# A decoder layer on one core: the first norm by halves, its second half on ScalarE, and the rotary tables late

## The chip, the cores and the metric

The kernel runs on one core of one Trainium2 chip. The metric is the device time of one execution in microseconds (us); the time before is the median of three runs. Engines: PE is TensorE (its queue of weight loads is PEld), DVE is VectorE, ACT is ScalarE, POOL is GpSimd, SP is SyncE, whose queue issues the DMAs here.

## The reference

The input x has 8 sequences of 128 tokens with 256 features. The layer is, with residual sums between its parts:

```
h = layernorm(x)
attention with 16 heads of 128 and 64 memory slots per head:
  q, k = rope(h Wq^T), rope(h Wk^T);  v = h Wv^T;  g = h Wg^T
  s = clip(h Ws1^T Ws2^T + bs2);  es = exp(s);  enz = 1 / cumsum(es over tokens)
  A = tril(q k^T) / sqrt(128);  ok = enz * (A es);  qv = softmax(ok)
  o = tril((qv * enz) es^T) v;  rmsnorm(o) * silu(g), then Wo
cross attention, 32 heads of 8, with a rotary embedding by positions that are an input
feed-forward: 8 experts, the best 2 by a gate, and a shared one
```

Everything is computed in float32. A product with a weight is made of three fp32r products: each side is split into a rounded high part and a low part (high*high + high*low + low*high).

## The kernel before

The tokens stand as 8 sequences in two halves of 4. The program has three stages.

**Start-up.** SP issues twelve DMAs in order: the first half of x, the constants, the second half of x, the positions, `ws1`, `wqk[0]`, `ws2`, `wvg[0]` and others. DVE computes the statistics of both halves (`Norm.vector_stats`, L289), POOL takes variance to the power -1/2 (L313), and DVE normalises both halves (`vector_norm`, L304, 8 instructions of 128x256). PE transposes each half into two PSUM banks (L322, 8 transposes a half). ACT rounds each bank to `ht_hi` (`Norm.scalar`, L330, 4 instructions), and DVE subtracts to `ht_lo` (`vector_low`, L337, 4 instructions). While it waits, PE turns the identity over (`keep_clocked`, L526 to 529): 22 times, 6 times and 10 times. Then PE multiplies both halves by `Ws1` (the slot inputs, 6 matmuls of 512 columns a half), and DVE makes `us` out of each half: it adds the constants from PSUM into `u_full` (L723), rounds it (L725, a copy) and joins high and low part (L727). PE waits before ST and SN until all of `us` is there.

**The attention.** The 16 heads are 8 pairs. Pair i of the attention runs beside the projections of pair i+1. Projections ("fills") are QK n (queries or keys of one head and one half: 6 matmuls into one bank), VG n (values and gates of one sequence), ST, SN (slot scores) and CS (cumulative sums, with `Ln` and `Exp` on ACT). An attention group g has the steps A, E, T, W, O, OT, Y. Each engine walks through a list of steps written by hand. For the projections of pair 0 and the attention of pair 0 the lists are `H_PE`, `H_DVE`, `H_ACT` and `H_POOL` (L153 to 184); an entry (step, n, i) belongs to attention pair i, and i = -1 means the projections of pair 0. `every_turn` (L243) walks through the head list and then repeats `PE_ORDER`, `DVE_ORDER`, `ACT_ORDER`, `POOL_ORDER` in a loop for five further pairs. `head_plan` (L226) gives the first 14 fills one of 8 banks each, then two banks in turn. A fill waits until its bank's last content is drained: QK by three DVE instructions (L796 to 798), VG by two of ACT (L884, L887) and one of DVE (L803), ST and SN by one of DVE (L809), CS by ACT's `Ln` (`summed`). The loop's first QK waits for the first CS of the pair before.

Before the logarithm of CS 0, ACT loads the table set with `Ln` (L835), and after CS 1 it loads `exp_and_others` again (L917); `Tanh` and `Exp` are both in that set. L741 is DVE's part of A, L771 of OT, L673 and L680 are the matmuls of ST and SN.

**The rotary tables** of the cross attention, which comes after the eighth pair, are computed in the head: `RA` (DVE, 14 small instructions, L364 to 381), `RS` (ACT, one `Sin`, which needs a table set of its own, L385), `RT` (DVE, 4 small instructions, L391 and 392). RA is the first step of `H_DVE`, RS stands after VG 3 in `H_ACT`, RT after VG 4 in `H_DVE`.

**Cross attention and feed-forward** follow in an order written by hand; the change does not touch them.

Of the kernel before, what the change touches and what calls it, by code (L numbers as in the profile page):

```python
# [275 lines left out]
class Norm:  # L276


    def __init__(self, nc, ctx, banks, xs, hn, ht_hi, ht_lo, ident, name):
# [6 lines left out]
        self.half_set, self.rstd_done, self.hn_done = sem("half_set"), sem("rstd_done"), sem("hn_done")  # L286
        self.turned, self.hi_done, self.lo_done = sem("turned"), sem("hi_done"), sem("lo_done")

    def vector_stats(self, dve, x_in):  # L289
        for half in range(2):  # L290
            seqs = slice(4 * half, 4 * half + 4)
            dve.wait_ge(x_in[half], 16)
            for b in range(4 * half, 4 * half + 4):
                dve.bn_stats(out=self.stats[:, b, :], in_=self.xs[:, b, :]).then_inc(self.stats_done, 1)
            for b in range(4 * half, 4 * half + 4):
                dve.wait_ge(self.stats_done, b + 1)
                dve.bn_aggr(out=self.mv[:, b, :], in_=self.stats[:, b, :]).then_inc(self.mv_done, 1)
            dve.wait_ge(self.mv_done, 4 * half + 4)
            dve.tensor_scalar(self.var_eps[:, seqs, 0], self.mv[:, seqs, 1], EPS, None, ALU.add).then_inc(self.var_done, 1)
# [15 lines left out]
    def tensor(self, pe, normalised_here=True, before=lambda half: None):  # L315
        for half in range(2):
            before(half)
            if normalised_here:
                pe.wait_ge(self.hn_done, 4 * half + 4)
# [1528 lines left out]
```

## Time and profile before

| | us |
|---|---|
| median of 3 runs (604.08, 606.02, 606.09) | 606.02 |
| profiled execution, its own time | 605.02 |
| span in its profile | 603.2 |
| PE busy | 578.4 (96%) |
| DVE busy | 485.5 (80%) |
| ACT busy | 371.6 (62%) |
| POOL busy | 282.4 (47%) |

The span is the time from the first to the last instruction of that execution; 1.8 us lie around it. Busy time of an engine is the time in which an instruction of it runs; matmuls are pipelined, so a busy PE is not PE at its peak.

### The profile page before, as it was taken

The page shows a single profiled execution, that of the slowest core. Times are in us where ns is not written, and L with a number is a line of the kernel's source. Part 1 is how long each engine was busy: PE and PEld are TensorE (multiplying, and loading weights), DVE is VectorE, ACT ScalarE, POOL GpSimd, SP SyncE. Part 2 cuts the span into 40 slices and gives each one's busy share as a digit, 9 for nine tenths or more (in the row PEclk, how much of TensorE's full clock was granted, in tenths as well). Part 3 has the DMA queues.
Part 4 walks back from the last instruction along what each step waited for, and adds up shares of the span by engine and source line. Part 5 has one row for each costly group of instructions (what it writes and reads, how often), then busy time and mean ns, then how long its engine had stood idle before and what let it go on. Part 6 is the DMA issues. An engine that isn't in the chain of part 4 may idle for free. (4 is left out here: it accounts for less than half of the span.)

```text
span 603.2 us, 14152 instructions
## 1 busy us (share of the span) xinstructions
PE 578.4 (96%) x4426; PEld 487.8 (81%) x4426; DVE 485.5 (80%) x1150; ACT 371.6 (62%) x1168; POOL 282.4 (47%) x324
## 2 busy tenths in 40 slices
PE   6989999999999999999999999998799999999997
PEld 5868888888888888888888788886578878877786
DVE  6999978977977977986987888687597887886766
ACT  3438557657657566656655576776867567566453
POOL 3367754845754663664675566355771220220000
PEclk9999999999999999999999999999989999999999
DMA  8200201100100200200200000231000000000000
GB/s 274 74 0 11 80 1 35 54 2 25 62 0 0 87 0 0 87 0 0 87 0 0 18 3 1 89 120 76 2 3 11 4 10 12 3 10 13 3 9 18
DMA packets 10321, 19.35 MB, mean 32 GB/s; under 512 B 2336, under 2 KB 5920, under 8 KB 10144
## 3 DMA queue, kind: packets, MB, share of 16 engines
q1 hardware_dynamic: 10272, 18.74, 9.2%
q8 instruction: 26, 0.43, 0.3%
q14 instruction: 23, 0.19, 0.1%
HBM read 17.55 MB, written 1.05 MB: 31 GB/s over the span
## 5 line engine op out<-in xcount | busy, mean ns | idle before, releaser
L884 ACT ACTIVATE sa_v<-bank 128x256 f32<-128x256 f32 x64 | 24.5, 383 | 60.7 <-PE bank L268 60.7
L857 ACT ACTIVATE sa_ex<-sa_okb,sa_minus_top 128x64 f32<-128x64 f32 x128 | 43.0, 341 | 28.7 <-DVE sa_minus_top L750 26.7
L947 POOL TENSOR_TENSOR sa_qt<-sa_rope_cos,sa_rope_sin 128x512 f32<-128x512 f32 x32 | 41.1, 1286 | 39.0 <-DVE sa_rope_sin L798 38.1
L266 PE MATMUL bank<-ht_hi,sa_qk_hi 128*128 128x512 f32 x128 | 55.2, 431 | 1.4 <-DVE sa_gate L803 0.8
L947 POOL TENSOR_TENSOR sa_kt<-sa_rope_cos,sa_rope_sin 128x512 f32<-128x512 f32 x32 | 41.2, 1288 | 26.6 <-DVE sa_rope_sin L798 26.6
L266 PE MATMUL bank<-sa_vg_hi,ht_hi 128*128 128x512 f32 x128 | 53.0, 414 | 0.5 <-DVE sa_rope_sin L798 0.5
L268 PE MATMUL bank<-sa_vg_hi,ht_lo 128*128 128x512 f32 x128 | 50.5, 395 | 0.0
L267 PE MATMUL bank<-sa_vg_lo,ht_hi 128*128 128x512 f32 x128 | 50.5, 395 | 0.0
L268 PE MATMUL bank<-ht_hi,sa_qk_lo 128*128 128x512 f32 x128 | 50.5, 394 | 0.0
L796 DVE TENSOR_TENSOR sa_rope_cos<-bank,con 128x512 f32<-128x512 f32 x64 | 44.0, 687 | 7.8 <-PE bank L268 6.8
L267 PE MATMUL bank<-ht_lo,sa_qk_hi 128*128 128x512 f32 x128 | 50.2, 392 | 0.0
L1521 DVE TENSOR_REDUCE xf_neg_top<-bank 128x4 f32<-128x512 f32 x64 | 40.4, 683 | 9.4 <-PE bank L1399 9.4
L797 DVE TENSOR_TENSOR sa_rope_sin<-bank,con 64x512 f32<-64x512 f32 x64 | 44.4, 693 | 0.9
L798 DVE TENSOR_TENSOR sa_rope_sin<-bank,con 64x512 f32<-64x512 f32 x64 | 43.7, 684 | 0.8
L1722 POOL TENSOR_TENSOR xf_rot<-xf_by_cos,xf_by_sin 128x256 f32<-128x256 f32 x16 | 12.1, 759 | 61.2 <-DVE xf_by_sin L1514 61.2
L953 POOL TENSOR_TENSOR sa_qe<-sa_ex,sa_enz 128x256 f32<-128x256 f32 x32 | 23.5, 734 | 34.7 <-ACT sa_ex L857 34.7
L266 PE MATMUL bank<-sa_wo_hi,sa_ogt_hi 128*128 128x256 f32 x128 | 37.7, 295 | 0.7 <-issue 0.7
L1620 ACT ACTIVATE xf_wt<-bank 128x512 f32<-128x512 f32 x64 | 34.1, 603 | 6.5 <-PE bank L1411 6.5
L869 ACT ACTIVATE sa_junk<-bank 128x128 f32<-128x128 f32 x128 | 33.7, 283 | 6.6 <-PE bank L620 6.6
L764 DVE SCALAR_TENSOR_TENSOR sa_og<-bank,sa_rms,sa_gate 128x128 f32<-128x128 f32 x128 | 35.8, 343 | 1.6 <-POOL sa_rms L966 1.4
L803 DVE SCALAR_TENSOR_TENSOR sa_gate<-sa_th,bank 128x256 f32<-128x256 f32 x64 | 26.4, 417 | 12.5 <-ACT sa_th L887 5.9
L267 PE MATMUL bank<-sa_wo_lo,sa_ogt_hi 128*128 128x256 f32 x128 | 36.1, 282 | 0.0
(207 smaller groups left out, 1836.4 us busy)
## 6 DMA issues: line engine op xcount, KB each, us to landing
sa_qk_raw<-in_wqk SPq DMA_DIRECT2D x8, 512.0 KB, 3.8
sa_vg_raw<-in_wvg SPq DMA_DIRECT2D x8, 512.0 KB, 3.2
sa_wo_raw<-in_wo SPq DMA_DIRECT2D x8, 256.0 KB, 2.7
xf_w_raw<-in_w SPq DMA_DIRECT2D x2, 640.0 KB, 9.1
xf_w_raw<-in_w SPq DMA_DIRECT2D x1, 1152.0 KB, 7.4
xs<-in_x SPq DMA_DIRECT2D x2, 512.0 KB, 4.6
hn<-in_w SPq DMA_DIRECT2D x2, 512.0 KB, 4.8
out<-xs SPq DMA_DIRECT2D x8, 128.0 KB, 1.7
```

Source lines behind the costliest of these rows:

```text
L266: pe.matmul(out, w_hi, m_hi, start=first, stop=False)
L267: pe.matmul(out, w_hi, m_lo, start=False, stop=False)
L268: return pe.matmul(out, w_lo, m_hi, start=False, stop=last)
L764: ins = dve.scalar_tensor_tensor(out=og[:, s, u, :], in0=ps_o[s][:, u * DK:(u + 1) * DK], scalar=rms[:, s, u:u + 1], in1=gate[:, b, h * DK ...
L796: dve.tensor_tensor(rope_cos[:, s, :].rearrange("p (b t) -> p b t", b=4), psv, cos4, ALU.mult)
L797: dve.tensor_tensor(rs[0:64], psv[64:128], sin4[64:128], ALU.mult)
L798: dve.tensor_tensor(rs[64:128], psv[0:64], sin4[0:64], ALU.mult).then_inc(draining, 1)
L857: ins = act.activation(ex[:, s, u, :], okb[:, s, u, :], ACT.Exp, bias=minus_top[:, s, u:u + 1], accum_out=total[:, buffer_of(i, g, 4), u:u ...
L869: ins = act.activation(junk[:, u, :], ps_o[s][:, u * DK:(u + 1) * DK], ACT.Square, scale=(EPS * DK) ** -0.5, accum_out=ss[:, s, u:u + 1])
L947: pool.tensor_tensor(dst[:, h, c * HALF:(c + 1) * HALF], rope_cos[:, s, :], rope_sin[:, s, :], ALU.add).then_inc(roped, 1)
L1521: dve.tensor_reduce(neg_top[:, b % 2, n % 4, 4 * (n // 4):4 * (n // 4) + 4], bank(filled(step, n, b), 0, 512, 4), AX.X, ALU.max, negate=Tr ...
L1620: act.activation(wt[:, n, :, :], bank(filled(step, n, b), 0, 512, 4), ACT.Exp, scale=XDIM ** -0.5).then_inc(exp_done, 1)
```

## The change

The statistics are taken and normalised half by half, and the second half is normalised by ACT (`Identity` with scale rstd and bias -mean*rstd, the latter from one new DVE instruction). PE transposes the first half after 14 turns instead of 22, makes the first half's slot inputs, and only then transposes the second half; the second half's slot inputs come after QK 0 and QK 1. DVE's rounding copy of `us` goes to ACT. DVE takes QK 0 and QK 1 before VG 0 and VG 1. RA moves to after Y 0 of pair 0, RS to after VG 7 and before CS 0 of the projections of pair 1, RT to the end of DVE's head list. ACT loads its first table set before it waits for anything, and rounds `wvg[0]` before the second half's transposes instead of after `ws2`. ST and SN wait only for the two low parts of `us`.

```diff
-H_DVE = [("RA", 0, -1), ("VG", 0, -1), ("VG", 1, -1), ("QK", 0, -1), ("QK", 1, -1), ("VG", 2, -1), ("VG", 3, -1),
-    ("SN", 0, -1), ("SN", 1, -1), ("VG", 4, -1), ("RT", 0, -1), ("QK", 2, -1), ("QK", 3, -1), ("VG", 5, -1),
+H_DVE = [("QK", 0, -1), ("QK", 1, -1), ("VG", 0, -1), ("VG", 1, -1), ("VG", 2, -1), ("VG", 3, -1), ("SN", 0, -1),
+    ("SN", 1, -1), ("VG", 4, -1), ("QK", 2, -1), ("QK", 3, -1), ("VG", 5, -1), ("VG", 6, -1), ("QK", 4, -1),
...
+    ("VG", 2, 0), ("QK", 6, 0), ("W", 3, 0), ("O", 2, 0), ("VG", 3, 0), ("ST", 1, 0), ("Y", 0, 0), ("RA", 0, -1),
+    ("OT", 1, 0), ("VG", 4, 0), ("VG", 5, 0), ("OT", 2, 0), ("O", 3, 0), ("Y", 1, 0), ("QK", 7, 0), ("VG", 6, 0),
+    ("Y", 2, 0), ("OT", 3, 0), ("VG", 7, 0), ("Y", 3, 0), ("RT", 0, -1)]
-H_ACT = [("VG", 0, -1), ("VG", 1, -1), ("VG", 2, -1), ("VG", 3, -1), ("RS", 0, -1), ("W2P", 0, -1), ("VG", 4, -1),
+H_ACT = [("VG", 0, -1), ("VG", 1, -1), ("VG", 2, -1), ("VG", 3, -1), ("W2P", 0, -1), ("VG", 4, -1), ("W2P", 0, 0),
...
+    ("OT", 3, 0), ("VG", 7, 0), ("RS", 0, -1), ("CS", 0, 0), ("CS", 1, 0)]
...
+    def vector_shift(self, dve):
+        dve.wait_ge(self.rstd_done, 2)
+        dve.scalar_tensor_tensor(out=self.shift[:, :], in0=self.mv[:, 4:8, 0], scalar=-1.0, in1=self.rstd[:, 4:8, 0],
+                                 op0=ALU.mult, op1=ALU.mult).then_inc(self.shift_done, 1)
+    def scalar_norm(self, act):
+        act.wait_ge(self.shift_done, 1)
+        for b in range(4, 8):
+            act.activation(self.hn[:, b, :], self.xs[:, b, :], ACT.Identity, bias=self.shift[:, b - 4:b - 3],
+                           scale=self.rstd[:, b, 0:1]).then_inc(self.second_done, 1)
...
# tensor (PE)
-        norm.tensor(pe, before=lambda half: keep_clocked((22, 6)[half]))
-        keep_clocked(10)
-        pe.wait_ge(ws1_lo_done, 1)
-        for half in range(2):
+        keep_clocked(14)
+        norm.tensor(pe, 0)
+        keep_clocked(18)
+        pe.wait_ge(ws1_lo_done, 1)
+        slot_inputs(0)
+        norm.tensor(pe, 1)
+        keep_clocked(2)
...
         def head_waits(step, n, i):
+            if (step, n, i) == ("VG", 0, -1):
+                slot_inputs(1)
...
# vector (DVE)
-        norm.vector_stats(dve, x_in)
+        norm.vector_stats(dve, x_in, 0)
         norm.vector_norm(dve, 0)
-        norm.vector_norm(dve, 1)
+        norm.vector_stats(dve, x_in, 1)
         dve.wait_ge(ws1_hi_done, 1)
         dve.tensor_tensor(ws1_lo[:, :, :], ws1_raw[:, :, :], ws1_hi[:, :, :].bitcast(F32), ALU.subtract).then_inc(ws1_lo_done, 1)
+        norm.vector_shift(dve)
         norm.vector_low(dve)
...
+        def slot_low(half):
+            dve.wait_ge(us_hi_done, half + 1)
...
+        slot_sums(0)
+        def slot_inputs_too(step, n, i):
+            if (step, n, i) == ("QK", 1, -1):
+                slot_low(0)
+                slot_sums(1)
+            elif (step, n, i) == ("VG", 0, -1):
+                slot_low(1)
...
# scalar (ACT)
+        act.preload_act_table_set("exp_and_others")
         act.wait_ge(con_in, 16)
+        act.activation(tri_r[:, :], tri, ACT.Copy).then_inc(tri_done, 1)
         act.wait_ge(ws1_in, 16)
-        act.activation(tri_r[:, :], tri, ACT.Copy).then_inc(tri_done, 1)
         act.activation(ws1_hi[:, :, :], ws1_raw[:, :, :], ACT.Copy).then_inc(ws1_hi_done, 1)
+        norm.scalar(act, (0, 1))
         act.wait_ge(qk_in, 16)
         act.activation(qk_hi[:, :, :], qk_raw[:, :, :], ACT.Copy).then_inc(qk_hi_done, 1)
-        norm.scalar(act)
+        norm.scalar_norm(act)
+        act.wait_ge(vg_in, 16)
+        act.activation(vg_hi[:, :, :], vg_raw[:, :, :], ACT.Copy).then_inc(vg_hi_done, 1)
+        norm.scalar(act, (2, 3))
         act.wait_ge(ws2_in, 16)
         act.activation(ws2[:, :, :], ws2_raw[:, :, :], ACT.Copy).then_inc(ws2_hi_done, 1)
-        act.wait_ge(vg_in, 16)
-        act.activation(vg_hi[:, :, :], vg_raw[:, :, :], ACT.Copy).then_inc(vg_hi_done, 1)
+        for half in range(2):
+            cols = slice(half * HALF, (half + 1) * HALF)
+            act.wait_ge(u_full_done, half + 1)
+            act.activation(us[:, cols], u_full[:, cols], ACT.Copy).then_inc(us_hi_done, 1)
```

## Rows read from the trace of the kernel before

**Rows 1.** Stretches: length, busy us of PE, PEld, DVE, ACT, POOL, granted clock, DMA.

```profile
30.00:50.00 20.00, 18.28 (x95) 14.44 (x95) 19.49 (x37) 9.54 (x25) 13.48 (x11) 1.00 0.00 0
100.00:340.00 240.00, 237.76 (x1540) 204.18 (x1539) 198.92 (x401) 146.75 (x513) 139.94 (x151) 1.00 0.08 28
430.00:445.00 15.00, 12.52 (x118) 9.16 (x117) 9.51 (x31) 11.34 (x29) 7.94 (x10) 0.77 0.02 5
```

**Rows 2.** Timeline, PE, start-up: start, us, instruction, count.

```profile
5.67 4.96 PE L529 MATMUL bank<-con 128*128 128x128 f32 x22 [5.67 <-DMA con<-in_constants]
...
12.53 1.04 PE L322 MATMUL bank<-con,hn 128*128 128x128 f32 x8
...
14.42 0.48 PE L266 MATMUL bank<-ht_hi,sa_ws_hi 128*128 128x512 f32 x1
...
17.26 0.39 PE L266 MATMUL bank<-ht_hi,sa_qk_hi 128*128 128x512 f32 x1
```

**Rows 3.** Timeline, DVE, POOL and ACT, start-up.

```profile
6.28 1.02 POOL L313 TENSOR_TENSOR norm_rstd<-norm_var_eps,norm_minus_half 128x4 f32<-128x4 f32 x1 [4.96 <-DVE norm_var_eps L299]
...
7.61 1.40 DVE L294 BATCH_NORM_STATS2 norm_stats<-xs 128x6 f32<-128x256 f32 x4 [1.49 <-DMA xs<-in_x]
...
9.41 2.83 DVE L304 TENSOR_SCALAR hn<-xs,norm_mv,norm_rstd 128x256 f32<-128x256 f32 x8
9.58 1.25 POOL L313 TENSOR_TENSOR norm_rstd<-norm_var_eps,norm_minus_half 128x4 f32<-128x4 f32 x1 [2.28 <-DVE norm_var_eps L299]
...
9.84 0.40 ACT L820 ACTIVATE sa_ws_hi<-sa_ws_raw 128x256 fp32r<-128x256 f32 x1
...
12.49 2.60 DVE L337 TENSOR_TENSOR ht_lo<-bank,ht_hi 128x512 fp32r<-128x512 f32 x4
```

**Rows 4.** Timeline, DVE, the rounding copies of the slot inputs.

```profile
17.29 1.86 DVE L725 CAST sa_us<-sa_gate 128x512 fp32r<-128x512 f32 x1
...
20.63 0.43 DVE L725 CAST sa_us<-sa_gate 128x512 fp32r<-128x512 f32 x1
```

**Rows 5.** Timeline, PE and DVE, from 21.7 to 31.4 us.

```profile
21.77 0.67 DVE L364 TENSOR_TENSOR rotary_angle<-rotary_pos,con 128x4 f32<-128x4 f32 x8
...
23.77 0.75 DVE L803 SCALAR_TENSOR_TENSOR sa_gate<-sa_th,bank 128x256 f32<-128x256 f32 x2
...
28.40 1.07 PE L680 MATMUL bank<-sa_ws_pair,sa_us 128*128 128x128 f32 x8
...
29.35 1.28 DVE L809 TENSOR_SCALAR sa_sn<-bank 128x512 f32<-128x512 f32 x2
...
30.88 0.18 DVE L391 COPY rotary_cos<-rotary_trig 128x32 f32<-128x32 f32 x1
...
31.34 0.69 DVE L796 TENSOR_TENSOR sa_rope_cos<-bank,con 128x512 f32<-128x512 f32 x1
```

**Rows 6.** Timeline, DVE and PE, around Y 0 and OT 2 of pair 0.

```profile
79.33 0.68 DVE L771 TENSOR_TENSOR sa_ogt_lo<-bank,sa_ogt_hi 128x512 fp32r<-128x512 f32 x1
81.51 0.42 DVE L803 SCALAR_TENSOR_TENSOR sa_gate<-sa_th,bank 128x256 f32<-128x256 f32 x1 [1.50 <-PE bank L268]
...
81.80 0.60 PE L632 MATMUL bank<-con,sa_og 128*128 128x128 f32 x4
```

**Rows 7.** Timeline, ACT, the table loads and what runs on them.

```profile
26.49 1.28 ACT L385 ACT_TABLE_LOAD   x1
27.78 0.26 ACT L385 ACTIVATE rotary_trig<-rotary_angle 128x64 f32<-128x64 f32 x1
...
90.61 1.28 ACT L835 ACT_TABLE_LOAD   x1
91.90 0.60 ACT L909 ACTIVATE sa_log_cs<-bank 128x512 f32<-128x512 f32 x1
```

**Rows 8.** Timeline, PE, the loop's first QK, and a wait at 430 us.

```profile
92.90 0.48 PE L266 MATMUL bank<-ht_hi,sa_qk_hi 128*128 128x512 f32 x1
...
433.25 0.41 PE L1446 MATMUL bank<-con,hn 128*128 128x128 f32 x2 [2.41 <-DVE hn L1553]
```

More of the change, by code:

```diff
@@ L286, in __init__, with vector_stats @@
         self.half_set, self.rstd_done, self.hn_done = sem("half_set"), sem("rstd_done"), sem("hn_done")
+        self.shift, self.shift_done, self.second_done = sb("shift", [P, 4]), sem("shift_done"), sem("second_done")
         self.turned, self.hi_done, self.lo_done = sem("turned"), sem("hi_done"), sem("lo_done")
-    def vector_stats(self, dve, x_in):
-        for half in range(2):
[L291 to L299, printed above, removed]
+    def vector_stats(self, dve, x_in, half):
+        seqs = slice(4 * half, 4 * half + 4)
+        dve.wait_ge(x_in[half], 16)
+        for b in range(4 * half, 4 * half + 4):
+            dve.bn_stats(out=self.stats[:, b, :], in_=self.xs[:, b, :]).then_inc(self.stats_done, 1)
+        for b in range(4 * half, 4 * half + 4):
+            dve.wait_ge(self.stats_done, b + 1)
+            dve.bn_aggr(out=self.mv[:, b, :], in_=self.stats[:, b, :]).then_inc(self.mv_done, 1)
+        dve.wait_ge(self.mv_done, 4 * half + 4)
+        dve.tensor_scalar(self.var_eps[:, seqs, 0], self.mv[:, seqs, 1], EPS, None, ALU.add).then_inc(self.var_done, 1)
+    def vector_shift(self, dve):
[7 more added lines that the diff above has]
+                           scale=self.rstd[:, b, 0:1]).then_inc(self.second_done, 1)
     def vector_norm(self, dve, half):
@@ L313, in pool, with tensor, scalar @@
             pool.tensor_tensor(self.rstd[:, seqs, 0], self.var_eps[:, seqs, 0], self.minus_half[:, seqs], ALU.pow).then_inc(self.rstd_done, 1)
[L315 to L319, printed above, removed]
-            for kc in range(KC):
-                for b in range(4):
-                    mm = pe.transpose(self.banks[2 * half + kc][:, b * TOK:(b + 1) * TOK],
-                                      self.hn[:, 4 * half + b, kc * P:(kc + 1) * P], self.ident)
-                mm.then_inc(self.turned, 1)
-    def scalar(self, act):
-        for n in range(4):
+    def tensor(self, pe, half):
+        pe.wait_ge(self.second_done if half else self.hn_done, 4)
+        for kc in range(KC):
+            for b in range(4):
+                mm = pe.transpose(self.banks[2 * half + kc][:, b * TOK:(b + 1) * TOK],
+                                  self.hn[:, 4 * half + b, kc * P:(kc + 1) * P], self.ident)
+            mm.then_inc(self.turned, 1)
+    def scalar(self, act, steps):
+        for n in steps:
             half, kc = n // 2, n % 2
@@ L529, in keep_clocked, with slot_inputs @@
                 pe.transpose(banks[7][:, 0:TOK], ident, ident)
-        norm.tensor(pe, before=lambda half: keep_clocked((22, 6)[half]))
-        keep_clocked(10)
-        pe.wait_ge(ws1_lo_done, 1)
-        for half in range(2):
+        def slot_inputs(half):
             pe.wait_ge(norm.hi_done, 2 * half + 2)
@@ L718, in vector, with slot_sums @@
                                  in1=ws2_raw[:, :, :], op0=ALU.mult, op1=ALU.add).then_inc(ws2_done, 1)
-        for half in range(2):
+        def slot_sums(half):
             cols = slice(half * HALF, (half + 1) * HALF)
@@ L800, in run @@
                     dve.wait_ge(th_done, 8 * r + n + 1)
+                    if isinstance(r, int) and r == 0 and n == 0:
+                        dve.wait_ge(us_done, 2)
                     if attend:
@@ L809, in run @@
                     dve.tensor_scalar(dst[:, n, :], ps[:, :], -CLAMP, CLAMP, ALU.max, ALU.min).then_inc(draining, 1)
-        return every_turn(dve, H_DVE, run, banks, {"RA": lambda: rotary.vector_angles(dve), "RT": lambda: rotary.vector_tables(dve)})
+        return every_turn(dve, H_DVE, run, banks, {"RA": lambda: rotary.vector_angles(dve), "RT": lambda: rotary.vector_tables(dve)},
+                          before=slot_inputs_too)
     def scalar(act):
@@ L926, in gpsimd @@
         norm.pool(pool)
-        pool.wait_ge(norm.hn_done, SEQS)
+        pool.wait_ge(norm.hn_done, 4)
         pool.wait_ge(qk_hi_done, 1)
```

10 lines of the change are left out of this document (4 added, 6 removed), and 22 rows, old and new, of tables (H_ACT, H_DVE).

## The prediction

> **What bounds the kernel now.** I read the table of busy stretches first. From 100 to 340 us PE is busy 237.76 of 240 us [rows 1]: there the loop runs, nothing but PE's own work counts, and a delay of PE at its entrance stays to the end. From 30 to 50 us it is different: PE 18.28 of 20 us, DVE 19.49 [rows 1]. DVE sets the pace there and PE loses 1.72 us waiting for drained banks. So the change can win in two places: before 17.26 us, where PE has not yet begun its projections [rows 2], and in DVE's chain from SN 0 at 29.35 us on [rows 5], where what DVE has less to do moves everything behind it. It can lose wherever it puts work in front of something that PE is about to want. I then followed the timeline of each engine through the start, around 80 us and into the loop.
>
> **Part 1: PE's start.** DVE may normalise the first half as soon as POOL's power is done, 6.28 + 1.02 = 7.30 [rows 3]. One of the 8 instructions takes 2.83 / 8 = 0.35, four 1.42: done at 8.8 instead of 10.83. The 14 turns last 14 x 4.96 / 22 = 3.2 us from 5.67 [rows 2], to 8.8 also; so the first transposes start 2.0 us earlier, at 8.85 instead of 10.84. They run at the slow pace (8 x 0.22 = 1.8), to 10.6, and the 18 turns that follow fill PE to about 12.8. All this is ahead of what is needed, for the next step is held by something else: `vector_low` stands on DVE behind the new shift, the shift behind the second rstd. DVE's second statistics start at 8.8 instead of 7.61; from 7.61 to the variance at 9.50 it took 1.9 (POOL starts at 9.58), so POOL starts at 10.75 and needs 1.02 to 1.25 [rows 3]: 11.9. The shift is a 128x4 instruction that the trace does not have; at least 0.1 and at most the 0.35 of a normalising one, I take 0.2: 12.1. Two of the four low parts take 2 x 2.60 / 4 = 1.3 [rows 3]: 13.5. Then PE: slot inputs of one half, half of 17.26 - 14.42 = 2.84, so 1.42 to 1.47; second transposes 0.9 to 1.04 and two turns 0.2 [rows 2]. QK 0 starts at 13.5 + 1.45 + 0.95 + 0.2 = 16.1, between 15.9 and 16.4, against 17.26.
>
> But the second half's slot inputs have only moved behind QK 1, and they are 1.42 us. From QK 0 to SN 0 it was 28.40 - 17.26 = 11.14 [rows 2, 5]; now it is 12.56, and SN 0 starts at 28.65 instead of 28.40. PE has gained nothing by then: +0.25, between 0 and +0.6.
>
> ACT's new work hides. Four normalising activations of 128x256: nearest is 0.40 for a 128x256 copy [rows 3], so at most 1.6, more likely 1.2 with overlap and no less than half of that; 12.1 + 1.6 = 13.7, and PE wants them at 14.95. The cover is 1.2 us; behind the wait for the shift ACT has vg's rounding queued, which POOL's low part and VG 0 need, but VG 0 comes only at 16.1 + 2.8 + 1.4 = 20.3. ACT then still has the two banks and ws2 to round (an estimate from the 0.40 of 256 columns: under 1 us for 512, under 1.6 for 1024), which puts `slot_sums(0)` on DVE at about 19. The first table load is hidden before the constants arrive.
>
> **Part 2: DVE until SN 0.** What goes from DVE: four normalising instructions 1.42; the copies 1.86 + 0.43 = 2.29 [rows 4]; RA, 21.77 to 23.77 = 2.0; RT, 30.88 to 31.34 = 0.46 [rows 5]. That is 6.2 us. Laid out in the new order: sums of half 0 until 19.9, QK 0 (three of 0.69) 2.1 until 22.0, low part 0 and sums 1 until 23.4, QK 1 until 25.6, low part 1 26.2, VG 0 to 3 until 27.9 (each 0.33 by 0.75 for two, the later two waiting a little for ACT's `Tanh`). PE needs sums 1 for VG 3's bank at about 24.5, which leaves 1.1 us. In the kernel before DVE came to SN 0 at 29.35, just behind PE's SN 0 (half of it done at 28.40 + 0.6 = 29.0). Now DVE is there at 27.9 and waits for PE: 28.65 + 0.6 = 29.25. So of 6.2 us only what was behind 29.35 counts, RT's 0.46, and 0.1 by which SN is taken sooner, with 0.2 to either side for PE's start. QK 2 starts at 30.8 instead of 31.34 [rows 5] and the chain DVE to PE is 0.5 us earlier until PE takes over at about 46. Bounds: -0.2 and, if SN came as soon as DVE is free, -1.9. I take -0.5.
>
> **Part 3: RA at 79 us.** It stands in front of OT 1 (79.33) and takes 2.0. DVE was idle 1.50 us before the gate at 81.51 [rows 6], so most of it is hidden. OT 1 ends at 81.33 + 0.68 = 82.0 instead of 80.0; PE's OT 2 was at 81.80 [rows 6] and waits for it. +0.25; the gates and OT 2's own drain follow within that. At least 0 (if the POOL-free spot makes it shorter), at most +1.5 (if some of its copy-like instructions wait for POOL as the copy of 1.86 did against 0.43 [rows 4]).
>
> **Part 4: RS and RT at the loop's entrance.** Before, ACT loads Sin's table (1.28), runs Sin (0.26) and loads back (1.28) at 26.5, where ACT is not what is waited for. Now it stands between VG 7 and CS 0. One load is saved, since CS 0 loads its set anyway; the other is not: the load at 90.61 becomes Sin's, 1.28 and 0.26 later comes the one for `Ln` [rows 7]. The first logarithm ended at 91.90 + 0.60 = 92.50; now 94.06, 1.56 later. The loop's first QK on PE waits for exactly this (its bank) and started at 92.90 [rows 8], so 0.40 was to spare: PE stands 1.56 - 0.40 = 1.16. What follows it there (DVE's QK drain, A 1, E 0) moves with it, and the other late results of ACT (second logarithm, the pair's slot weights) are late by the same 1.56, so at most 0.4 more. Nothing gives it back, because the loop is PE's [rows 1]. Lower bound 0, if PE has other work to run ahead of the wait; the lists show none. RT hides behind this: DVE waits for Sin until about 92.2 with only the loop's A 0 queued behind it, and that needs PE's A 0, which ends just before 92.90. I take +1.15.
>
> The Trainium skill, "ScalarE: Activation LUTs", section "What ACT_TABLE_LOAD costs", says that a change of the table set costs 2.66 us, 1.28 for the load and about as much again for a drain. Here the load is 1.28 and the next activation starts 0.01 later (26.49, 1.28, 27.78) [rows 7]; by the page's figure the entrance would cost about 2.5 instead of 1.15 and the sum would be 1.4 higher. I go by the rows.
>
> **Sum.** -0.5 + 0.25 + 1.15 = +0.9. On the profiled execution, 605.02, it is 605.9; the median shown, 606.02, lies 1.0 above that execution and the lowest run 0.9 below it, so I predict between 605.9 and 606.9: 606.4.
>
> **Rivals.**
> (a) The likeliest, +0.9, with its own range from -0.5 to +2.2: 605 to 608. Chance 0.66.
> (b) DVE's relief carries through. The 6.2 us are really off an engine that was busy 19.49 of 20 us [rows 1], and if PE's QK 0 at 16.1 instead of 17.26 could be kept, PE's 1.72 us of waiting would go too. That gives up to -1.2 - 1.7 = -2.9, and with RT and a hidden Sin -3.4: 602.6. Against it: the 1.42 us of slot inputs only moved. Chance 0.05; half of it below 603.
> (c) The Sin is hidden at the loop's entrance or PE's wait is absorbed: -0.5 + 0.25 = -0.25, 605.3, decided by whether the first QK of the loop still starts 0.8 behind A 0. Chance 0.14.
> (d) Slower: PE's clock. The turns before 10.8 run at 4.96 / 22 = 0.23 each, the later transposes at 1.04 / 8 = 0.13 [rows 2], the two levels of 1.2 and 2.4 GHz. Later the granted clock falls for a while: mean 0.77 in 430 to 445 us, so 0.23 x 15 x 2 = 6.9 us at the lower level, after PE had stood 2.41 us [rows 1, 8]. In the new order PE waits once more in the start, some 0.7 us from 12.8 to 13.5. If that takes the clock away, or lets it rise later than now, everything up to SN 0 that falls in such a stretch runs at half pace: 3.4 us for 6.9. With +0.9 that is +4.3: 609.5 to 610.5. It decides from the point at which PE's wait comes near 2.4 us; I see 0.7 and no more than 1.3. The Trainium skill ("TensorE: Matmul & The Clock Gate", "What's actually happening") says the same in general, that the clock follows how busy the array has lately been; it gives no reason to expect a fall here. Chance 0.07.
> (e) RA meets POOL's work, and the late slot weights cost their 0.4: +0.9 + 1.3 + 0.4 = +2.6, 608.1. Chance 0.08.
> The stretches at the lower clock after 430 us may also fall otherwise once all is shifted by 1 us; that is the likely source of the 2 us between the three runs, and it goes into the range.
>
> **How the numbers follow.** 0.5% is 3.0 us, about what can be told from no change. Faster by more than that needs (b) whole: 0.04. Slower needs (d), or (e) with a bad run: 0.08. The rest, 0.88, is no change. The range that holds eight in ten is that of (a), (c) and (e) with 1 us of scatter between runs: 604.0 to 608.6.
>
> **What would show it.** PE's first transposes at 8.9, first slot-input matmul at 13.4 to 13.6, QK 0 at 16.1, SN 0 at 28.65; DVE idle about 1.3 us before SN 0 and QK 2 at 30.8; from there to 79 us each row 0.5 earlier. A wait of PE of about 0.2 before OT 2 of pair 0, and one of about 1.2 before the loop's first QK, released by ACT's logarithm, with an extra table load of 1.28 before it. The prediction is wrong if PE has no wait at the loop's entrance, if the low parts come well before 13.4, or if PE's clock falls before 30 us.

## The result and the profile after

The changed kernel took 606.26 us (median of 12 runs, 604.48 to 610.22) against 605.07 (602.63 to 606.09, 12 runs) for the kernel before: ratio 1.0037 with a 95% interval of 1.002 to 1.0054. Within 0.5% is what was predicted as "no change", and 606.26 lies 0.1 from the 606.4 of the forecast. The difference of the two medians is +1.2 us and the ratio says +2.2 (1.2 to 3.3 by its interval), where the sum said +0.9. That the time itself comes within 0.1 is partly luck: the forecast started from 605.5 (606.4 - 0.9) for the kernel before, which is 0.4 more than it now measures, and added 0.3 less than the medians show. The profiled execution took 606.32 us with a span of 604.5, against 605.02 and 603.2.

The stretches, as in [rows 1] (start and end; length; busy us and instructions of PE, PEld, DVE, ACT, POOL; granted clock; DMA share; GB/s):

```profile
30.00:50.00 20.00, 18.66 (x100) 14.89 (x98) 19.24 (x32) 9.82 (x24) 13.83 (x11) 1.00 0.00 1
100.00:340.00 240.00, 237.79 (x1543) 204.22 (x1542) 198.81 (x400) 147.63 (x520) 139.60 (x150) 1.00 0.08 28
422.00:430.00 8.00, 7.67 (x118) 5.89 (x116) 3.76 (x9) 5.45 (x13) 6.81 (x9) 0.57 0.00 0
430.00:445.00 15.00, 10.17 (x104) 7.23 (x103) 10.79 (x32) 12.75 (x33) 7.35 (x10) 1.00 0.01 3
```

In the loop nothing has changed (237.79 against 237.76 busy). From 30 to 50 us PE is busy 0.38 us more and DVE 0.25 less. The lower clock that the kernel before had from 430 to 445 us falls elsewhere in this execution: from 422 to 430 us the granted clock is 0.57, and from 430 to 445 it is 1.00, although PE stands there as long as it did before [rows 8], before this row of the timeline:

```profile
436.75 0.41 PE L1486 MATMUL bank<-con,hn 128*128 128x128 f32 x2 [2.40 <-DVE hn L1593]
```

The timeline of the changed kernel, rows of PE, DVE, ACT and POOL in the start, which answer to [rows 2, 3, 5] (start, us, engine, line, instruction, count, and in brackets the idle time before it and what ended it):

```profile
8.80 1.43 PE L332 MATMUL bank<-con,hn 128*128 128x128 f32 x8 [0.26 <-DVE hn L317]
...
11.78 0.16 DVE L304 SCALAR_TENSOR_TENSOR norm_shift<-norm_mv,norm_rstd 128x4 f32<-128x4 f32 x1 [0.91 <-POOL norm_rstd L326]
...
11.98 2.08 ACT L311 ACTIVATE hn<-xs,norm_shift,norm_rstd 128x256 f32<-128x256 f32 x4
12.01 2.37 POOL L969 TENSOR_TENSOR sa_qk_lo<-sa_qk_raw,sa_qk_hi 128x1024 fp32r<-128x1024 f32 x1 [0.27 <-ACT sa_qk_hi L857]
13.29 0.47 PE L266 MATMUL bank<-ht_hi,sa_ws_hi 128*128 128x512 f32 x1 [1.08 <-DVE ht_lo L347]
...
15.77 0.48 PE L266 MATMUL bank<-ht_hi,sa_qk_hi 128*128 128x512 f32 x1
...
25.02 1.85 POOL L987 TENSOR_TENSOR sa_kt<-sa_rope_cos,sa_rope_sin 128x512 f32<-128x512 f32 x1 [1.59 <-DVE sa_rope_sin L828]
...
28.37 0.89 PE L696 MATMUL bank<-sa_ws_pair,sa_us 128*128 128x128 f32 x7
28.96 1.29 DVE L841 TENSOR_SCALAR sa_sn<-bank 128x512 f32<-128x512 f32 x2 [1.19 <-PE bank L696]
...
30.50 0.68 DVE L826 TENSOR_TENSOR sa_rope_cos<-bank,con 128x512 f32<-128x512 f32 x1
```

QK 0 starts 1.49 us earlier than before, SN 0 only 0.03: the slot inputs of the second half stand between them. DVE is idle for 1.19 us before SN 0, so most of what was taken from it bought nothing. Its QK 2 is 0.84 earlier (31.34 before), but 5 us later its gate (L835, at 35.44) waits 0.28 for ACT's `Tanh`.

The same view later, PE, DVE, ACT and POOL, which answer to [rows 6 to 8]:

```profile
78.84 0.66 DVE L374 TENSOR_TENSOR rotary_angle<-rotary_pos,con 128x4 f32<-128x4 f32 x8
...
80.20 1.10 POOL L1006 TENSOR_TENSOR sa_rms<-sa_msq,sa_minus_half 128x4 f32<-128x4 f32 x1
80.21 0.23 DVE L385 SCALAR_TENSOR_TENSOR rotary_angle<-rotary_turns,rotary_angle 128x64 f32<-128x64 f32 x1
...
81.67 0.63 PE L648 MATMUL bank<-con,sa_og 128*128 128x128 f32 x4 [0.20 <-DVE sa_ogt_lo L801]
...
90.53 1.28 ACT L395 ACT_TABLE_LOAD   x1
91.82 0.26 ACT L395 ACTIVATE rotary_trig<-rotary_angle 128x64 f32<-128x64 f32 x1
92.09 1.28 ACT L875 ACT_TABLE_LOAD   x1
93.39 0.60 ACT L949 ACTIVATE sa_log_cs<-bank 128x512 f32<-128x512 f32 x1
...
94.12 0.50 PE L266 MATMUL bank<-ht_hi,sa_qk_hi 128*128 128x512 f32 x1 [1.06 <-ACT sa_log_cs L949]
```

PE's first QK of the loop starts at 94.12 instead of 92.90, behind two table loads in a row where there had been one.

To see where PE gains or loses, I set the start of each matmul against that of the same matmul of the kernel before (offset, in us; both profiled executions). For the changed kernel it is -0.09 at 30 us, -0.48 at 45, -0.10 at 83 (behind OT 2), +1.25 at 101 and +1.26 at 400. Behind 400 us the offset wanders by more than 2 us with the stretches at the lower clock, which fall differently in each execution; medians of 6 to 12 runs are therefore good to about 1 us, and the offset at 101 says more about the head.

### The profile page after: what moved, and what is told of

Its sections match the earlier page's. It is cut to its first block and busy times, and to the rows that moved or that the text cites. A ratio compares the mean times of both kernels' runs of the same rounds, so it can differ in the third digit from the quotient of the medians.

```text
span 604.5 us, 14143 instructions
## 1 busy us (share of the span) xinstructions
PE 577.0 (95%) x4422; PEld 485.8 (80%) x4422; DVE 481.7 (80%) x1145; ACT 373.2 (62%) x1173; POOL 282.4 (47%) x324
## 3 DMA queue, kind: packets, MB, share of 16 engines
HBM read 17.55 MB, written 1.05 MB: 31 GB/s over the span
## 5 line engine op out<-in xcount | busy, mean ns | idle before, releaser
L268 PE MATMUL bank<-sa_wo_hi,sa_ogt_lo 128*128 128x256 f32 x128 | 36.1, 282 | 0.0
```

The source lines that it names most:

```text
L268: return pe.matmul(out, w_lo, m_hi, start=False, stop=last)
```

## The experiments

All offsets in one place (PE against the kernel before, as above), with the times:

| kernel | at 30 | 45 | 83 | 101 | median us (range, runs) | ratio to before |
|---|---|---|---|---|---|---|
| changed, first | -0.09 | -0.48 | -0.10 | +1.25 | 606.26 (604.48 to 610.22, 12) | 1.0037 [1.002, 1.0054] |
| changed, again | +3.49 | +3.11 | +3.51 | +4.86 | 608.07 (604.13 to 612.9, 12) | 1.006 [1.003, 1.0089] |
| e1 rotary early | +6.97 | +7.75 | +7.73 | +7.73 | 612.15 (607.51 to 613.1, 6) | 1.0115 [1.0084, 1.0147] |
| e2 only rotary late | -0.30 | -0.69 | -0.26 | +1.05 | 605.75 (603.99 to 606.56, 12) | 1.0023 [1.0008, 1.0038] |
| e3 rotary hidden | +1.65 | +1.28 | +1.27 | +1.27 | 608.45 (607.32 to 610.0, 6) | 1.0078 [1.0055, 1.0101] |
| f1 POOL waits for shift | -0.01 | -0.40 | 0.00 | +1.33 | 606.67 (604.13 to 608.02, 12) | 1.0039 [1.0024, 1.0053] |
| f2 no sine table | +0.41 | +0.02 | +0.42 | +0.44 | 605.5 (602.99 to 606.61, 12) | 1.0011 [0.9996, 1.0026] |
| f3 best of changed | -0.05 | -0.44 | -0.46 | -0.46 | 604.57 (602.3 to 606.44, 12) | 0.9995 [0.9979, 1.0011] |
| f4 rotary covered, on before | -0.43 | -0.81 | -0.83 | -0.83 | 604.18 (602.52 to 605.3, 12) | 1.0003 [0.9989, 1.0016] |
| g1 low parts first | -0.34 | -0.70 | -0.70 | -0.68 | 605.07 (601.98 to 606.14, 12) | 1.0003 [0.9983, 1.0023] |
| h1 shift behind POOL | +2.48 | +2.11 | +2.10 | +2.10 | 604.52 (602.31 to 607.36, 12) | 1.0007 [0.999, 1.0025] |
| i1 rounding back on DVE | +2.08 | +1.69 | +2.07 | +3.41 | 608.29 (606.44 to 609.31, 6) | 1.0066 [1.0041, 1.0091] |
| j1 held but clocked | +3.20 | +2.80 | +3.23 | +4.56 | 608.97 (606.87 to 609.96, 10) | 1.0073 [1.0054, 1.0092] |

**The changed kernel again.**

> The changed kernel once more, as the measure for the others of this call. Theory (the time was lost at two places, in front of the loop and before OT 2, and only half a microsecond was won before): +1.3 us on the kernel before, rows from 100 us on later by 1.2 to 1.3; the first QK of the loop waits 1.0 to 1.1 us for ACT's logarithm, OT 2 of pair 0 0.2 for DVE. Rival (the 2.2 us of the ratio come from somewhere else, the granted clock at the start or after 430 us): the median moves by more than 1.6 while the rows from 100 to 400 us stay at +1.3.

The profile of this run was another one than the first. Its timeline around the new shift, and a row of its stretches:

```profile
11.82 2.33 POOL L969 TENSOR_TENSOR sa_qk_lo<-sa_qk_raw,sa_qk_hi 128x1024 fp32r<-128x1024 f32 x1
11.88 2.29 DVE L304 SCALAR_TENSOR_TENSOR norm_shift<-norm_mv,norm_rstd 128x4 f32<-128x4 f32 x1 [0.91 <-POOL norm_rstd L326]
...
15.52 0.77 PE L266 MATMUL bank<-ht_hi,sa_ws_hi 128*128 128x512 f32 x1 [3.55 <-DVE ht_lo L347]
16.08 0.63 PE L267 MATMUL bank<-ht_lo,sa_ws_hi 128*128 128x512 f32 x1
...
19.28 0.47 PE L266 MATMUL bank<-ht_hi,sa_qk_hi 128*128 128x512 f32 x1
```

```profile
14.80:18.20 3.40, 2.68 (x6) 2.04 (x7) 0.57 (x1) 2.43 (x5) 0.89 (x1) 0.52 0.49 154
```

An instruction on 4 columns takes 2.29 us: it starts 0.06 behind POOL's subtraction and ends with it. I call this a hold: the shift is held by POOL's instruction. In the first profile it started 0.23 ahead of POOL and took 0.16. With it the low parts (from 14.10 instead of 11.86) and ACT's normalising (from 14.21 instead of 11.98) are 2.2 late, PE has stood 3.55 us, and then its matmuls of 512 columns run at 0.63 instead of 0.39: granted clock 0.52 in this stretch, the 1.2 GHz level, where it was 1.00 from 12.0 to 14.8. QK 0 is 3.51 later than in the first profile. Six of these 12 runs lay between 608.9 and 612.9, and 3 of the first 12 between 608.9 and 610.2. The same program gave both profiles, so which of the two instructions comes first differs from execution to execution; that the upper group of runs is the executions with the hold is not shown yet, and f1 tests it.

**e1: the rotary steps back at their old places.**

```diff
+H_DVE: ("RA", 0, -1) before ("QK", 0, -1);  ("RT", 0, -1) after ("VG", 4, -1)
+H_ACT: ("RS", 0, -1) after ("VG", 3, -1)
```

> The changed kernel with RA, RS and RT back at the places of the kernel before (RA first in DVE's head list, RS after VG 3, RT after VG 4). Theory: both waits go (1.06 and 0.20, with the reopening of PE's pipeline 1.6 us), but RA's 2.0 us now exceed DVE's idle 1.19 before SN 0 and hold back the sums of half 1 that VG 3's bank needs, about 0.8, and RT's 0.46 comes back; QK 2's first DVE instruction at 31.6 to 31.8 instead of 30.50. Against the kernel before: -0.1 to +0.5, that is 1.0 faster than the changed kernel. Rival (DVE's 6.2 us of relief matter as a whole): RA early costs its full 2.0 and the kernel is as slow as the changed one or slower, +1.3 or more on before.

The expectation missed. The profile shows a held shift as well, and two further waits; the waits of PE from 11 to 90 us (for whom: us in total, times, longest), and one stretch:

```profile
PE bank L696 <- ACT sa_ws_pair L883: 1.7, 1, 1.7
PE bank L266 <- DVE sa_gate L742: 0.7, 1, 0.7
```

```profile
36.00:40.00 4.00, 4.00 (x12) 3.13 (x12) 3.91 (x11) 0.76 (x2) 0.15 (x1) 0.59 0.00 0
```

With the hold, QK 0 is at 19.54, 3.8 behind the first profile of the changed kernel. Behind it RA delays the sums of the second half, `Sin`'s table load stands in front of the pair's slot weights, and the clock falls a second time. What each of these is worth was not tested apart. The waits at OT 2 and at the loop's entrance are gone, as the theory wanted (7.73 at 83 and at 101), but in the new order the rotary steps cannot stay where they were: even the fastest run took 607.51.

**e2: only the rotary steps late, on the kernel before.**

```diff
 (kernel before)
+H_DVE: ("RA", 0, -1) after ("Y", 0, 0);  ("RT", 0, -1) at the end
+H_ACT: ("RS", 0, -1) after ("VG", 7, 0)
```

> The kernel before with one part of the change alone: RA after Y 0, RS after VG 7, RT at the end of DVE's head list. Theory: DVE is 0.35 earlier at SN 0 (then it waits for PE's SN 0 at 28.4) and RT's 0.46 goes, so about the same 0.5 won at 45 us as in the changed kernel; the wait in front of the loop 1.0 to 1.1 and that before OT 2 0.2. Rows from 100 us on +1.2 to +1.3, the same as the changed kernel: the rearranged start is worth nothing. Rival (the rearranged start earns the half microsecond): rows at 45 us unchanged or later than before, rows from 100 us on +1.6 or more.

Its constants landed 0.25 earlier than in the profile of before, and the offset at 17 us is -0.25. Taken from there: -0.44 at 45, then +0.43 at OT 2 and +1.31 at the entrance, together +1.30. For the changed kernel, without a held shift, the same is +1.25. So the rebuilt start with all its other edits earns nothing over moving three steps, and DVE's gain of 0.45 comes from the rotary work that leaves the start.

**e3: RA in DVE's gap before the second low parts, RS where ACT has time.**

```diff
-        norm.vector_low(dve)
+        norm.vector_low(dve, (0, 1))
         dve.wait_ge(con_in, 16)
+        rotary.vector_angles(dve)
+        norm.vector_low(dve, (2, 3))
+H_ACT: ("RS", 0, -1) before ("QKHI", 0, -1), with a load of exp_and_others behind it
```

> The changed kernel with RA in DVE's idle stretch at 13.1 to 16.0 us (between the low parts of the two halves), RS with both its table loads in ACT's idle stretch before QKHI (36.5 to 41.8 us), RT left at the end of DVE's head list. Theory: RA (2.0) fits into 2.88, the loads and Sin (1.28 + 0.26 + 1.28 = 2.8) into 5.28, both waits are gone: rows from 100 us on -0.4 to -0.6 against before, 1.7 faster than the changed kernel. If RA's small copies wait for POOL's low part of qk, which runs until 14.4, RA ends at about 15.7, still inside. Rival (the wait in front of the loop has another cause than the Sin, such as the cumulative sums): it stays, rows +0.9 or more.

The entrance came out as expected (1.27 at 83 and at 101), the gap did not. Its timeline, DVE and POOL:

```profile
12.39 2.39 POOL L971 TENSOR_TENSOR sa_qk_lo<-sa_qk_raw,sa_qk_hi 128x1024 fp32r<-128x1024 f32 x1 [0.54 <-ACT sa_qk_hi L859]
13.16 2.15 DVE L374 TENSOR_TENSOR rotary_angle<-rotary_pos,con 128x4 f32<-128x4 f32 x8
...
15.23 2.40 POOL L974 TENSOR_TENSOR sa_vg_lo<-sa_vg_raw,sa_vg_hi 128x1024 fp32r<-128x1024 f32 x1 [0.42 <-ACT sa_vg_hi L862]
15.34 2.33 DVE L378 TENSOR_SCALAR rotary_angle<-rotary_angle 128x32 f32<-128x32 f32 x1
```

RA's eight small additions take 2.15 instead of 0.67 and the instruction after them 2.33 instead of 0.18, held until a subtraction of POOL is over (POOL ends at 14.78 and 17.63, DVE at 15.31 and 17.67). The last, a `TENSOR_SCALAR`, is held although it has only one tensor in SBUF as its input. The low parts of DVE, which read PSUM and SBUF, run beside the same POOL instructions at their usual length (1.28 for two, at 11.86 in the changed kernel's first profile).

**f1: POOL begins its first subtraction only after the shift.**

```diff
         pool.wait_ge(norm.hn_done, 4)
+        pool.wait_ge(norm.shift_done, 1)
```

> The changed kernel with one wait more: POOL's low part of qk (2.3 us) starts only after DVE's shift. In the slow profile of the changed kernel the 128x4 shift took 2.29 us instead of 0.16 and ended when POOL's instruction did, and PE stood 3.55 us, after which its clock was halved for 3.4 us. Theory (DVE's shift is held when POOL's long instruction is under way first, and it is chance which of them starts first): the shift is 0.16 in the profile, no run of the twelve or so lies above 607.5, the median is 605.5 to 606.3, and the rows from 100 us on are +1.2 to +1.4 later than before, start-up scatter of 0.4 aside. Rival (the slow third of the runs is the clock's own doing at the start): runs above 608.5 stay, three or more of twelve.

The shift takes 0.17 in the profile. The highest of 12 runs is 608.02, where the changed kernel had 3 and 6 of 12 at 608.9 and above: the upper group is gone, and with it the rival. The changed kernel was not timed again beside f1, so this rests on none of 12 runs against 9 of 24. The rest missed by a little: four runs are above the 607.5 I had set as a limit, the median, 606.67, is above the 605.5 to 606.3, and its ratio of +1.45 to +3.2 us stands above the +1.33 of the offset. That last 1 us does not come from the head. In f1's own profile the offset is still +1.33 at 400 us and +2.60 at 600. And where both kernels had a mean granted clock of 0.997, f1 took 605.22 and 605.23 against a median of 603.80 in 13 executions of the kernel before, +1.4. Seven of f1's 12 runs were at 0.992, against 9 of 35 before; whether that is chance or f1's doing stays open.

**f2: f1 with the `Sin` as a copy, without its table set.**

```diff
-        act.activation(self.trig[:, :, :, :], self.angle[:, :, :, :], ACT.Sin).then_inc(self.trig_done, 1)
+        act.activation(self.trig[:, :, :, :], self.angle[:, :, :, :], ACT.Copy).then_inc(self.trig_done, 1)
```

> The kernel f1 with the Sin replaced by a Copy at the same place, so that no table set of its own is loaded (the rotary tables are wrong). Theory (the wait in front of the loop is the extra table load of 1.28 and Sin): it falls from 1.06 to nothing, PE's first QK of the loop starts 0.8 behind A 0, 1.2 to 1.3 us are won on f1 and the wait of 0.2 before OT 2 stays; rows from 100 us on 0.0 to +0.1 against before. Rival (the wait comes from RT on DVE or from ACT's order): at least 0.6 of it stays.

The timeline at ACT's first logarithm and at PE's first QK of the loop, and DVE and POOL before:

```profile
25.04 1.88 DVE L748 SCALAR_TENSOR_TENSOR sa_us<-sa_us,con,sa_gate 128x512 fp32r<-128x512 f32 x1
...
25.09 1.28 POOL L988 TENSOR_TENSOR sa_kt<-sa_rope_cos,sa_rope_sin 128x512 f32<-128x512 f32 x1 [1.59 <-DVE sa_rope_sin L828]
...
91.18 1.28 ACT L875 ACT_TABLE_LOAD   x1
...
93.34 0.48 PE L266 MATMUL bank<-ht_hi,sa_qk_hi 128*128 128x512 f32 x1
```

Without the second load PE does not wait at the entrance (from 83 to 101 the offset moves by 0.02, in f1 by 1.33). The whole cost there is that one load. The offset from 100 us on was expected at 0.0 to +0.1 and is +0.44; 0.4 of it stands there ahead of the entrance already (+0.41 at 30) and is another hold. DVE's joining of the low part and POOL's addition began within 0.05 us of each other, and DVE took 1.88 instead of 0.75, POOL its usual 1.28. In the changed kernel's first profile the same pair went the other way: DVE 0.75 (at 24.98), POOL 1.85 [its row at 25.02]. In both profiles DVE's start is recorded first, by 0.04 and 0.05 us, so at this distance the recorded starts do not tell who is held.

**f3: f1 with RA behind OT 1 and RS behind SN 1.**

```diff
+H_DVE: ("RA", 0, -1) after ("OT", 1, 0)
+H_ACT: ("RS", 0, -1) after ("SN", 1, 0), with a load of exp_and_others behind it
```

> The kernel f1 with the rotary parts where they are covered: RA after OT 1 instead of before it, RS after SN 1 of pair 0's attention, followed at once by the load back (1.28 + 0.26 + 1.28 = 2.8 us in ACT's idle 2.9 from 84.1 to 87.0), RT at the end as in the changed kernel. Theory: no wait before OT 2, none in front of the loop; rows from 100 us on -0.4 to -0.6 against before and 1.8 ahead of f1. Rival (relief of DVE is worth more once the waits are gone): -1.5 or better.

Its timeline, ACT and PE:

```profile
83.89 1.28 ACT L395 ACT_TABLE_LOAD   x1
...
85.46 1.28 ACT L959 ACT_TABLE_LOAD   x1
...
90.14 1.28 ACT L875 ACT_TABLE_LOAD   x1
...
92.44 0.48 PE L266 MATMUL bank<-ht_hi,sa_qk_hi 128*128 128x512 f32 x1
```

ACT loads one table more than the changed kernel, and it costs PE nothing, for its offset is -0.46 at 83 and at 101. Both late waits are gone and the offset stays at -0.46.

**f4: the same rotary places on the kernel before.**

```diff
 (kernel before)
+H_DVE: ("RA", 0, -1) after ("OT", 1, 0);  ("RT", 0, -1) after ("Y", 3, 0)
+H_ACT: ("RS", 0, -1) after ("SN", 1, 0), with a load of exp_and_others behind it
```

> The kernel before with only the rotary parts moved to the same covered places as in f3. Theory (the rearranged start is worth nothing; the half microsecond is RT's 0.46 and DVE's catching up at SN 0): rows from 100 us on -0.4 to -0.6, the same as f3 within 0.2, and no run above 606.5 since the shift does not exist. Rival (the start earns part of it): f4 at 0 to -0.2 and f3 ahead of it by 0.4 or more.

Its start lies 0.38 earlier by its constants; the rest, -0.45, equals f3, and no run is above 605.3. Neither is told from the kernel before by its median.

**g1: f3 with the first low parts ahead of the shift.**

```diff
-        norm.vector_shift(dve)
-        norm.vector_low(dve)
+        norm.vector_low(dve, (0, 1))
+        norm.vector_shift(dve)
+        norm.vector_low(dve, (2, 3))
 turns: 18 -> 14 ahead of slot_inputs(0), 6 more behind it
```

> The kernel f3 with the first half's two low parts on DVE ahead of the shift (POOL's low part of qk still waits for the shift), 14 turns instead of 18 ahead of the first slot inputs and 6 between them and the second transposes. Theory (the first slot inputs wait only for the low parts, which wait only for the shift): first slot-input matmul at 12.3 instead of 13.3, but the second transposes then wait for ACT's half, shift 12.2, 2.08 of activations, 14.4; so QK 0 at 15.6, only 0.2 ahead of f3; rows from 100 us on 0.2 ahead of f3, -0.6 to -0.7 against before. Rival (the start is worth its whole microsecond): QK 0 at 14.8, -1.4 against before.

QK 0 at 15.52 against 15.81 in f3, and 0.2 at 101: the size expected, too little for the median.

**h1: g1 without f1's wait, so that POOL can begin first.**

```diff
-        pool.wait_ge(norm.shift_done, 1)
```

> The kernel g1 without POOL's wait for the shift: now the shift is ready at about 12.2 and POOL's 2.4 us instruction on qk is usually under way at 12.0. Theory (DVE's small instruction with two inputs in SBUF is held until POOL's long one ends): the shift takes 1.9 to 2.3 us in the profile, ends with POOL's instruction, ACT's normalising starts that much later, PE stands 2 us in front of the second transposes; 2.0 to 3.6 us slower than g1, the upper end where PE's clock falls for 3.4 us. Rival (the long shift was an accident of the recording or of DVE's queue): the shift 0.16, time as g1.

The timeline of the profiled execution, POOL, DVE and PE:

```profile
11.93 2.39 POOL L971 TENSOR_TENSOR sa_qk_lo<-sa_qk_raw,sa_qk_hi 128x1024 fp32r<-128x1024 f32 x1
12.05 2.29 DVE L304 SCALAR_TENSOR_TENSOR norm_shift<-norm_mv,norm_rstd 128x4 f32<-128x4 f32 x1
...
16.50 1.09 PE L332 MATMUL bank<-con,hn 128*128 128x128 f32 x8 [1.93 <-ACT hn L311]
```

The hold is there, with QK 0 at 17.57 against 15.52 in g1, and PE's clock stays whole although it stood 1.93. But the time missed: 2.0 to 3.6 us more than g1 were expected, and the median, 604.52, is not above g1's 605.07. The order of the two is not forced here, and the runs show that the profiled execution was not the usual one: it took 607.36, the longest of the 12, and two others with the same mean granted clock of 0.994 took 604.30 and 604.77. A difference of 2.6 to 3.1 is about the offset between h1 and g1 at 101 us (2.10 + 0.68 = 2.8), so those two had no hold.

**i1: f1 with the rounding of `us` back on DVE.**

```diff
+            dve.wait_ge(u_full_done, half + 1)
+            dve.tensor_copy(us[:, cols], u_full[:, cols]).then_inc(us_hi_done, 1)
             dve.wait_ge(us_hi_done, half + 1)
 (ACT's two copies are gone)
```

> The kernel f1 with the rounding of the slot inputs back on DVE (two copies of 0.43 instead of ACT's 0.63). Theory (DVE's relief before SN 0 counts for nothing while PE is behind it: DVE waits 1.2 us there): both copies together 0.9 to 1.0 fit into that, QK 2's first DVE instruction moves by at most 0.1, rows from 100 us on as f1 within 0.15. If a copy meets POOL's addition for the rotated keys it is held up to 1.3 and 0.4 of it could show. Rival (the relief counts): +0.9 on f1.

Missed: 2.1 us at 30 instead of next to nothing. Its timeline, DVE, POOL, ACT and PE:

```profile
21.64 0.43 DVE L748 CAST sa_us<-sa_gate 128x512 fp32r<-128x512 f32 x1
21.76 1.46 POOL L986 TENSOR_TENSOR sa_qt<-sa_rope_cos,sa_rope_sin 128x512 f32<-128x512 f32 x1 [3.85 <-DVE sa_rope_sin L830]
22.10 1.66 DVE L750 SCALAR_TENSOR_TENSOR sa_us<-sa_us,con,sa_gate 128x512 fp32r<-128x512 f32 x1
...
29.19 0.38 ACT L925 ACTIVATE sa_th<-bank 128x256 f32<-128x256 f32 x1 [4.30 <-DVE sa_gate L837]
...
30.46 0.75 PE L696 MATMUL bank<-sa_ws_pair,sa_us 128*128 128x128 f32 x5 [1.52 <-ACT sa_ws_pair L881]
```

The copies cost 0.43 each, but they let POOL begin its rotation first, and the instruction behind them is held each time, 1.66 and 1.67 instead of 0.75: 2.7 in all. DVE's first gate, at 25.94 in f1, starts at 28.73. I had set this against the 1.2 us that DVE waits before SN 0, but the path that gives way first is another one: ACT's `Tanh` waits for that gate, the rounding of the pair's slot weights (`sa_ws_pair`) stands behind it on ACT, and PE's SN 0 needs these. In f1 they were done at 27.52 and SN 0 started at 28.45, so only 0.9 was to spare; here PE stands 1.52. So moving the rounding to ACT is worth about 2 us in the changed order, and not by its 0.86 of copies.

**j1: the shift always held, but PE kept turning.**

```diff
         dve.wait_ge(self.rstd_done, 2)
+        dve.wait_ge(qk_hi_done, 1)
+        dve.tensor_scalar(self.later[:, :], self.mv[:, 4:8, 0], -1.0, None, ALU.mult)
         dve.scalar_tensor_tensor(out=self.shift ...
-        keep_clocked(18)
+        keep_clocked(42)
```

> Changed kernel; DVE takes the shift only after ACT's rounding of wqk and one more 128x4 instruction, so that POOL's qk_lo always starts first and holds it, as it did in the first repeat of the changed kernel; and PE turns the identity over 42 times instead of 18 before the slot inputs, so that it stands about 0.3 us instead of 3.5. Which part of the +3.6 us is the held shift and which the clock? Theory (hold about 2.1, clock the rest): the shift takes about 2.2 us again, low parts at 14.2, PE's first slot-input matmul at 15.5 as in the repeat, but the granted clock stays 1.00 there, the six matmuls take 1.45 us instead of 2.7, and QK 0 starts at 18.1 instead of 19.28; PE in the loop +3.7 to the kernel before instead of +4.9; median 607 to 609 with no run at 612. Rival (the clock falls for another reason than PE's standing, such as what DVE, POOL and the DMAs do at that time): clock about 0.5 from 14.8 to 18.2 here as well, QK 0 at 19.3, in the loop +4.9.

Timeline and stretch:

```profile
12.42 2.37 POOL L972 TENSOR_TENSOR sa_qk_lo<-sa_qk_raw,sa_qk_hi 128x1024 fp32r<-128x1024 f32 x1 [0.70 <-ACT sa_qk_hi L860]
12.46 2.34 DVE L307 SCALAR_TENSOR_TENSOR norm_shift<-norm_mv,norm_rstd 128x4 f32<-128x4 f32 x1
...
16.15 0.47 PE L266 MATMUL bank<-ht_hi,sa_ws_hi 128*128 128x512 f32 x1 [0.87 <-DVE ht_lo L350]
...
18.62 0.48 PE L266 MATMUL bank<-ht_hi,sa_qk_hi 128*128 128x512 f32 x1
```

```profile
14.80:18.20 3.40, 2.53 (x17) 2.02 (x16) 1.20 (x3) 3.02 (x5) 0.28 (x2) 1.00 0.51 155
```

Up to the slot inputs everything is 0.6 later than I had written, since ACT's rounding of `wqk` and the added instruction came later. The offset of +4.56 at 101, where I had written +3.7, has 0.4 more: the joining of the second half was held here too (1.88, at 27.82). PE stood 0.87 and not 3.55 in front of the slot inputs, and the clock is decided for this stretch: 1.00 where it had been 0.52. Two of the 10 runs, 606.87 and 607.58, even had a mean granted clock of 1.000. From the first slot-input matmul to QK 0 it is 2.47 (18.62 - 16.15) against 3.76 in the repeat (19.28 - 15.52). Of the 3.5 us of an execution with the hold, 1.3 are the clock's, and 2.2 the held instruction's. In the runs it is no better than the changed kernel (606.87 to 609.96). The lowest is 4.2 us above the lowest of the kernel before beside it, 602.69, so the hold seems to be in every one of them now.

## Why the prediction was right, and where it was not

**Part 1, PE's start: right in mechanism where the shift is not held, a little off in size.** First transposes 8.80 (8.85), first slot inputs 13.29 (13.5), QK 0 15.77 (16.1, between 15.9 and 16.4), SN 0 28.37 (28.65). So PE came to SN 0 at -0.03 where I had +0.25, between 0 and +0.6; both lie just below their ranges. ACT's normalising took 2.08 and not the 1.6 I had as its upper bound; it hid nevertheless, done at 14.06 where PE came at 14.76.

**Part 2, DVE: right.** It idles 1.19 before SN 0 (1.3 predicted) and is 0.84 earlier at QK 2 (0.5 predicted), of which 0.48 is left at 45 us (-0.5 in the sum).

**Part 3, RA at 79 us: right, a little small.** From 78 to 83 us PE's offset goes from -0.49 to -0.10, +0.39 where the sum had +0.25. f3, with RA one step later, has none of it.

**Part 4, the loop's entrance: right in mechanism and nearly in size.** +1.35 from 83 to 101, where the sum had +1.15; f2 and f3 show that it is the one table load that is no longer covered. The load took 1.28 and the logarithm began 0.02 later; PE stood 1.06. The 2.66 that the Trainium skill gives ("ScalarE: Activation LUTs", section "What ACT_TABLE_LOAD costs") would have cost 1.4 more, and these runs do not show it.

**The step that was mis-sized is the shift in part 1**: "a 128x4 instruction that the trace does not have; at least 0.1 and at most the 0.35 of a normalising one". It measures 0.16 when it is first and 2.29 when POOL is first, in a race that is open to within 0.25 us. The row that warned of it was in my hands: the copy of 1.86 against 0.43, from 17.29 to 19.15 [rows 4]. This is what POOL did then in the kernel before:

```profile
16.23 2.64 POOL L932 TENSOR_TENSOR sa_vg_lo<-sa_vg_raw,sa_vg_hi 128x1024 fp32r<-128x1024 f32 x1 [1.37 <-ACT sa_vg_hi L827]
```

I used the row as a bound for RA at 79 us and not for the one new DVE instruction of the start, which stands right beside POOL's subtraction of 2.3 us. At 79 us it did no harm, though POOL was not idle: its 128x4 power ran from 80.20 for 1.10, and RA's instructions beside it took their usual 0.23. The Trainium skill says that POOL shares its SBUF interfaces with VectorE, with contention for DVE instructions that run in a 2-port perf mode or have two SBUF inputs ("GPSIMD Engine Reference", section "8. Key points"). The shift has two SBUF inputs, and the held profiles agree with the page; the low parts, with one input in PSUM, are not touched. The held copy and the held `TENSOR_SCALAR` have only one SBUF input each; in which mode they ran no run here shows. RA's two-input instructions beside the power do not fit the sentence as it stands. In these runs the contention is no slowing in proportion, but a hold to the end of the other's instruction.

**Rival (d) came true in part.** PE's clock did fall in the start, though by no wait of 0.7 as I looked at there: the held shift makes it 3.55. A fall of the clock before 30 us was one of my three signs of a wrong prediction, so for the executions with the hold the prediction is wrong, and a median over both kinds hides it. I had set the chance of (d) at 0.07 and its end at 609.5 to 610.5; 3 and then 6 of 12 executions were at 608.9 and above. Its rule, that it decides near a wait of 2.4 us, did not hold up either: the changed kernel stood 2.40 us before 436.75 and kept the clock. Rivals (b) and (c) failed: QK 0's lead was gone by SN 0, and PE has nothing to run ahead with at the entrance. Rival (e) failed too: RA took its 2.0 us.

The sum for an execution without the hold, +0.9, stands against +1.25 measured (-0.48 + 0.39 + 1.35, within 0.01). The runs agree: without those at 608.9 and above, the first 12 have a median of 606.16, 1.1 above the kernel before, and the second 12 one of 605.7, 1.0 above it. An execution with the hold costs 3.6 more at PE in the one I saw, so the rest of the ratios comes mainly from these; how often they occur is not known better than 9 in 24.

## What to carry to other kernels

Before adding a small DVE instruction that reads only SBUF, look up what POOL does at that moment. If POOL is in a long elementwise instruction on SBUF, price the small one at what is left of that and not at its own length, and settle by a wait or by the order which of them goes first. A step that is "moved to where there is room" is priced at its new place with everything it issues, table loads included; here the same load cost PE nothing at 84 us and 1.3 us at 92. And work taken from an engine counts only as far as its next meeting with the engine that sets the pace: of 6.2 us taken from DVE, 0.5 arrived. Work given back to it is measured against the shortest slack on all paths that it feeds: in i1 that was 0.9 by way of ACT, not the 1.2 in front of SN 0.
